# Spreading the last chunk's layer-1 tiles among the remaining layer-2 tiles in a two-layer dense graph kernel

## What is computed

```python
h = relu(layernorm(x))
mask = (adj < 0.5) & ~eye
S = where(mask, exp(-(1/r - 1/mu)**2 / (2*sigma**2)), 0)      # r = adj where mask, else 1
x = x + S @ (h @ W0 + B0)
h = relu(layernorm(x))
out = x + (adj*adj + eye) @ (h @ W1.T)
```

## Time and profile before

| | |
|---|---|
| median of 3 executions | 1946.03 us (1943.99 to 1946.5) |
| profiled execution | 1945.05 us, span 1943.3 us |
| PE / DVE / ACT / POOL busy, share of the span | 97% / 86% / 86% / 4% |
| mean granted TensorE clock | 0.994 of full speed |
| moved by DMA | 487.60 MB, mean 251 GB/s |
| layer-2 tiles: own / in chains; `adj` loads | 94 / 162; 418 |

### The profile page before, as it was taken

One profiled execution on the slowest core, in us unless ns is written; L12 is line 12 of the kernel. 1 busy time (PEld: TensorE's weight loads), 2 busy tenths in 40 slices (PEclk: granted clock), 3 DMA queues, 4 the chain that ended last, 5 costly groups with the idle time before them and its releaser, 6 DMA issues.

```text
span 1943.3 us, 12915 instructions
## 1 busy us (share of the span) xinstructions
PE 1876.0 (97%) x4576; PEld 842.4 (43%) x4576; DVE 1666.1 (86%) x937; ACT 1674.8 (86%) x963; POOL 83.0 (4%) x157
## 2 busy tenths in 40 slices
PE   6988989999999999999999999999999999999998
PEld 4543333344444444444444444444444444444443
DVE  7998999999999999999999999999999994333344
ACT  7999999999999999999999999999999994222221
POOL 0000000000000101010000000000000000000000
PEclk9999999999999999999999999999999999999999
DMA  7565676777787777776656564546564646889885
GB/s 269 190 233 204 249 279 243 256 268 270 265 318 297 294 286 293 288 275 246 257 216 227 207 226 178 218 175 241 205 240 153 227 173 249 313 335 323 329 326 195
DMA packets 77744, 487.60 MB, mean 251 GB/s; under 512 B 9968, under 2 KB 10352, under 8 KB 24176
## 3 DMA queue, kind: packets, MB, share of 16 engines
q1 hardware_dynamic: 65520, 446.92, 62.7%
q0 software_dynamic: 12160, 39.86, 5.6%
HBM read 464.72 MB, written 22.02 MB: 250 GB/s over the span
## 4 chain that ended last, share of the span: by engine, by line
ACT 65%; PE 24%; DVE 5%; issue 5%; DMA 1%; DVEq 0%; POOLq 0%; POOL 0%; SPq 0%
ACT rings L617 21%; ACT rings L627 20%; ACT rings L622 19%; PE p_x L369 17%; ACT rings L634 3%; PE p_l1b L355 3%; PE p_own L369 2%; DVE rings L495 2%; DVE rings L502 2%; DVE rings L513 1%; PE p_l1a L355 1%; DMA x_buf<-xT 1%; ACT rstd_buf L663 0%; ACT rstd_buf L661 0%; ACT square_buf L655 0%
## 5 line engine op out<-in xcount | busy, mean ns | idle before, releaser
L502 DVE SCALAR_TENSOR_TENSOR rings<-rings,small 128x2048 f32<-128x2048 f32 x256 | 600.9, 2347 | 58.8 <-ACT rings L622 58.0
L495 DVE SCALAR_TENSOR_TENSOR rings<-rings 128x2048 f32<-128x2048 f32 x256 | 585.3, 2286 | 0.6
L369 PE MATMUL p_x<-rings,h 128*128 128x512 f32 x1296 | 568.5, 592 | 0.1
L627 ACT ACTIVATE rings<-rings,small 128x2048 f32<-128x2048 f32 x256 | 532.6, 2080 | 4.1 <-DVE rings L502 4.1
L513 DVE TENSOR_TENSOR rings<-rings 128x2048 f32<-128x2048 f32 x174 | 397.9, 2287 | 147.0 <-PE p_x L369 146.6
L617 ACT ACTIVATE rings<-rings,small 128x2048 f32<-128x2048 f32 x256 | 509.0, 1988 | 7.6 <-DVE rings L495 6.9
L355 PE MATMUL p_l1b<-rings,h 128*128 128x512 f32 x1024 | 465.4, 599 | 27.8 <-ACT rings L627 27.8
L622 ACT ACTIVATE rings<-rings 128x2048 f32<-128x2048 f32 x256 | 487.9, 1906 | 4.9
L355 PE MATMUL p_l1a<-rings,h 128*128 128x512 f32 x1024 | 464.1, 598 | 12.5 <-ACT rings L627 12.5
L369 PEld LDWEIGHTS p_x<-rings,h 128*128 128x128 f32 x1296 | 246.3, 190 | 309.6 <-issue 309.1
L369 PE MATMUL p_own<-rings,h 128*128 128x512 f32 x752 | 338.3, 593 | 0.3
(11 more groups left out here) (69 smaller groups left out, 307.4 us busy)
## 6 DMA issues: line engine op xcount, KB each, us to landing
rings<-adjT SPq DMA_DIRECT2D x418, 1024.0 KB, 5.4
xa_buf<-acc_dram POOLq DMA_DIRECT2D x57, 256.0 KB, 6.5
acc_dram<-xa_buf POOLq DMA_DIRECT2D x52, 256.0 KB, 5.4
x_buf<-xT SPq DMA_DIRECT2D x32, 256.0 KB, 5.2
outT<-xa_buf POOLq DMA_DIRECT2D x16, 256.0 KB, 3.8
acc_dram<-y_buf POOLq DMA_DIRECT2D x15, 256.0 KB, 5.5
y_buf<-acc_dram POOLq DMA_DIRECT2D x11, 256.0 KB, 6.1
acc_dram<-x_buf POOLq DMA_DIRECT2D x1, 256.0 KB, 5.5
```

The costliest lines, as they stand in the source:

```text
L369: last = pe.matmul(out[:, :], h2[:, it.source * G + g, :], block_of(q_ring, it.m % Q_RING, g), start=(it.first and g == 0), stop=(it.last ...
L495: dve.scalar_tensor_tensor(out=tile(s_ring, t % S_RING), in0=tile(a_ring, slot), scalar=CUTOFF, in1=tile(a_ring, slot), op0=ALU.is_lt, op1 ...
L502: dve.scalar_tensor_tensor(out=v, in0=v, scalar=neg_2c, in1=v, op0=ALU.add, op1=ALU.mult).then_inc(squared, 1)
L627: act.activation(v, v, ACT.Exp, bias=exp_bias, scale=neg_k).then_inc(sens_done, 1)
```

## The change

Four things. The quotas of chunks 1 to 14 add up to 157 instead of 152. In the last chunk nearly all that is left goes among the sixteen layer-1 tiles: 65 items, four or five a step, three more (TAIL) right behind. The 31 tiles of sources 14 and 15 form the final chains, two tiles each (one for row 15); the first four are open together in four banks (`p_x[0]`, `p_x[1]`, `p_own[0]`, `p_l1[0]`), first their tiles of source 14, then those of source 15, and later ones use these four banks in turn. From the last chunk on ACT and DVE square in turn, and the steps between the layers come ahead of the squares. A chain is added after the DVE's part of the item three behind its last (one behind in final chains), and POOL's transfers are sorted by item instead of by step. The plan has 72 chains instead of 68, 90 own tiles instead of 94, 422 loads instead of 418; 17 chains end in chunks 4 to 8 instead of 30. ACT squares 39 items in chunks 1 to 14 instead of 37, DVE 19 in chunks 1 to 3 instead of 15.

```diff
-QUOTA = [0, 4, 7, 9] + [12] * 12
+QUOTA = [0, 5, 9, 11] + [12] * 11
+TAIL = 3
+OPEN = 4
+EVAC = 3
+STEAL = 0.5
...
+def slots_of(c):
+    if c == 1:
+        n = QUOTA[1]
+        return [H2_STEP + k * (NC - H2_STEP) // n for k in range(n)]
+    if c < NC - 1:
+        n = QUOTA[c]
+        return [(2 * k + 1) * NC // (2 * n) for k in range(n)]
+    n = NC * NC - 2 * NC + 1 - sum(QUOTA) - TAIL
+    return [(2 * k + 1) * NC // (2 * n) for k in range(n)] + [NC + k for k in range(TAIL)]
...
+    ends = [Chain(row, [J for J in range(NC) if (row, J) not in done], True) for row in range(NC)]
+    chains += ends
+    tail = [(ch, ch.sources[0]) for ch in ends[:OPEN]] + [(ch, ch.sources[1]) for ch in ends[:OPEN]]
+    tail += [(ch, J) for ch in ends[OPEN:] for J in ch.sources]
+    items += [Item(ch.row, J, ch, S_STEPS + TAIL + k) for k, (ch, J) in enumerate(tail)]
+    for k, ch in enumerate(chains):
+        ch.index = k
+        ch.bank = (k - len(chains) + NC) % OPEN if ch.final else k % 2
...
-    if it.step >= S_STEPS:
+    if it.step >= S_STEPS - NC:
         it.by = "act" if it.m % 2 else "dve"
...
+for ch in CHAINS:
+    ch.evac = max(ch.last_m + (1 if ch.final else EVAC), CHAINS[ch.index - 1].evac if ch.index else 0)
+    ch.store = ch.evac + 0.5
+    EVAC_AFTER.setdefault(min(ch.evac, len(ITEMS) - 1), []).append(ch)
+    TRANSFERS.append((ch.store, 0, ch.index))
+    if state_before(ch) is not None:
+        free = CHAINS[ch.index - XA_RING].store if ch.index >= XA_RING else 0
+        free = max([free, ch.first_m - 1] + [o.store for o in ch.before])
...
+        TRANSFERS.append((free, 1, ch.index))
+    ch.after = [o for o in CHAINS[:ch.index] if o.bank == ch.bank]
...
+        p_chain = p_x + [p_own[0], p_l1[0]]
...
-                elif it.first and it.chain.index >= 2:
-                    pe.wait_ge(xa_added, it.chain.index - 1)
+                elif it.first and it.chain.final and it.chain.bank == 2 and it.chain.row < OPEN:
+                    pe.wait_ge(y_ready, NC - 2)
+                elif it.first and it.chain.final and it.chain.bank == 3 and it.chain.row < OPEN:
+                    pe.wait_ge(x1_added, NC - 1)
+                elif it.first and it.chain.after:
+                    pe.wait_ge(xa_added, it.chain.after[-1].index + 1)
...
+                if c >= NC - 1:
+                    row_steps(c, i)
                 for it in AT_STEP[s]:
                     if it.by == "dve":
                         square_adj(it)
+                    for ch in EVAC_AFTER.get(it.m, []):
+                        add_chain(ch)
```

More of the change, by code:

```diff
@@ L23, with __init__ @@
 TINY = 2.0 ** -60
-QUOTA = [0, 4, 7, 9] + [12] * 12
+QUOTA = [0, 5, 9, 11] + [12] * 11
 S_STEPS = NC * NC
 H2_STEP = 9
+TAIL = 3
+OPEN = 4
+EVAC = 3
+STEAL = 0.5
 class Chain:
-    def __init__(self, index, row, sources, final):
-        self.index, self.row, self.sources, self.final = index, row, sources, final
+    def __init__(self, row, sources, final):
+        self.row, self.sources, self.final = row, sources, final
 class Item:
@@ L42, in __init__, with next_chain @@
         self.own = chain is None
-def best_row(c, limit, done):
+def slots_of(c):
[7 more added lines that the diff above has]
+    return [(2 * k + 1) * NC // (2 * n) for k in range(n)] + [NC + k for k in range(TAIL)]
+def next_chain(c, places, done):
     found = None
+    late = places[0] >= H2_STEP
+    limit = c if late and c < NC - 1 else c - 1
     for row in range(NC):
+        if row == c or row == c - 1 and not late:
+            continue
         left = [J for J in range(limit) if (row, J) not in done]
-        if row in (c - 1, c) or not left:
+        if not left:
             continue
-        key = (row < c, len(left), -row if row < c else row)
+        key = -(STEAL * (row > c) + 1 / len(left)), -row if row < c else row
         if found is None or key > found[0]:
@@ L54, in best_row @@
     return found
[L57 to L66, removed]
-def make_plan():
[L70 to L80, removed]
-            chains.append(chain)
[L82 to L94, removed]
-        rest = iter(J for J in range(NC) if J not in own)
[L96 to L106, removed]
@@ new lines, in make_plan @@
+def make_plan():
+    done, chains, items, order = set(), [], [], [list(range(NC))]
+    for c in range(1, NC):
+        places = slots_of(c)
+        own = [J for J in range(c) if (c, J) not in done][-len(places):]
+        steps = sorted({i for i in places if i < NC})
+        own_at = {steps[(2 * k + 1) * len(steps) // (2 * len(own))]: J for k, J in enumerate(own)}
+        own_at.pop(max(own_at))
+        own_at[NC - 1 if NC - 1 in steps else steps[-1]] = own[-1]
+        done.update((c, J) for J in own)
+        free, picked, taken = [], [], set()
+        for i in places:
+            if i in own_at and i not in taken:
+                taken.add(i)
+                picked.append((i, c, own_at[i], None))
+            else:
+                free.append(i)
+        while free:
+            _, row, left = next_chain(c, free, done)
+            left = left[:len(free)]
+            chain = Chain(row, left, False)
+            chains.append(chain)
+            done.update((row, J) for J in left)
+            picked += [(i, row, J, chain) for i, J in zip(free, left)]
+            free = free[len(left):]
+        rest = iter(J for J in range(NC) if J not in own)
+        order.append([own_at[i] if i in own_at else next(rest) for i in range(NC)])
+        picked.sort(key=lambda p: p[0])
+        items += [Item(row, J, chain, c * NC + i) for i, row, J, chain in picked]
+    ends = [Chain(row, [J for J in range(NC) if (row, J) not in done], True) for row in range(NC)]
[6 more added lines that the diff above has]
+        ch.bank = (k - len(chains) + NC) % OPEN if ch.final else k % 2
@@ L107, in make_plan @@
     return chains, items, order
 CHAINS, ITEMS, ORDER = make_plan()
-STEPS = S_STEPS + len([it for it in ITEMS if it.step >= S_STEPS])
+STEPS = ITEMS[-1].step + 1
 AT_STEP = [[] for _ in range(STEPS + 8)]
@@ L149 @@
     mine = [it for it in ITEMS if it.chain is ch]
-    ch.begin, ch.end, ch.last_m = mine[0].step, mine[-1].step, mine[-1].m
+    ch.begin, ch.end, ch.first_m, ch.last_m = mine[0].step, mine[-1].step, mine[0].m, mine[-1].m
     ch.before = [x for x in CHAINS[:ch.index] if x.row == ch.row]
@@ L179, with first_item @@
 PRIORS = [c for c in range(NC) if prior_of(c) is not None]
+EVAC_AFTER, TRANSFERS = {}, []
+for ch in CHAINS:
[6 more added lines that the diff above has]
+        free = max([free, ch.first_m - 1] + [o.store for o in ch.before])
+        if ch.begin >= (ch.row + 1) * NC:
+            free = max(free, [it.m for it in ITEMS if it.step >= (ch.row + 1) * NC + 4][0] + 0.2)
+        assert free <= ch.evac, (ch.row, ch.sources, free, ch.evac)
+        TRANSFERS.append((free, 1, ch.index))
+    ch.after = [o for o in CHAINS[:ch.index] if o.bank == ch.bank]
+def first_item(step):
+    return [it.m for it in ITEMS if it.step >= step][0]
+for c in range(NC):
+    TRANSFERS.append((first_item(NC * (c + 1) + 4) + 0.1, 2, c))
+    if c in PRIORS:
+        TRANSFERS.append((first_item(NC * c + 13), 3, c))
+TRANSFERS.sort()
 def gnn_program(nc, xT, adjT, W0, B0, mu, sigma, W1T, outT):
@@ L335, in _ @@
                     load_residual(c)
[L336 to L340, removed]
+                if s < S_STEPS and S_LOAD[s] >= n:
+                    load_tile(S_LOAD[s])
+                    n = S_LOAD[s] + 1
+                for it in AT_STEP[s]:
+                    if it.load >= n:
+                        load_tile(it.load)
+                        n = it.load + 1
                 if 2 <= s < NC:
@@ L580, in add_chain, with row_steps @@
                     dve.wait_ge(xa_loaded[k % XA_RING], 16 * loads)
-                    dve.tensor_tensor(buf[:, :], p_x[k % 2][:, :], buf[:, :], ALU.add).then_inc(xa_added, 1)
+                    dve.tensor_tensor(buf[:, :], p_chain[ch.bank][:, :], buf[:, :], ALU.add).then_inc(xa_added, 1)
+            def row_steps(c, i):
+                if c > NC:
+                    return
+                if i == 3:
+                    add_x1(c - 1)
+                if i == 4 and c >= 2:
+                    add_y(c - 1)
+                if i == 7:
+                    norm_row(c - 1)
             for s in range(STEPS + 8):
@@ L597, in _ @@
                         constants()
[L598 to L607, removed]
+                if 1 <= c < NC - 1:
+                    row_steps(c, i)
         @block.scalar
@@ L668, in keep_h2, with row_steps @@
                                ACT.Copy).then_inc(h2_ready, 1)
+            def row_steps(s):
+                c, i = divmod(s, NC)
+                if i == 5 and c <= NC:
+                    square_row(c - 1)
+                if i == 6 and c <= NC:
+                    rstd_row(c - 1)
+                if i == 8 and c < NC or s == S_STEPS + 7:
+                    keep_h2(c - 1)
             for s in range(STEPS + 8):
```

(11 more changed lines are left out.)

6 lines of the change are left out of this document (4 added, 2 removed).

## The result

The changed kernel takes **1930.02 us** (median of 6 executions, 1929.39 to 1930.87) against 1945.99 for the kernel before (now six executions, 1943.99 to 1946.5): a ratio of 0.9919, interval 0.9908 to 0.993, 16.0 us less. The forecast was 1928.3, with a range of 1923.5 to 1936. The profiled execution took 1930.87 us (span 1929.1), the slowest of the six.

A forecast was written before the change was run, and what follows sets the result against it. ScalarE was taken to pace the chunks up to the last and TensorE the rest; -18.5 (late part) + 0 (final pairs) + 0 (state transfers) + 0.8 (early chunks) = -17.7 us, forecasting 1928.3 us, range 1923.5 to 1936.

The forecast's parts named there:

- What bounds: Whole kernel: ScalarE paces the chunks up to the last, TensorE the rest.
- The late part: Layer-1 tile 238 to the last matmul: 425.4 us becomes 406.9, five tiles (17.2) and 1.4 us idle, 18.5 less.
- The covers costed at nothing: Last chunk: squares, row work and h2 copy stay hidden behind TensorE; a failed cover costs up to 3 us, once.
- The final pairs: Chains of two tiles at the end: VectorE's add and square cost nothing; bound 7.6 us for eleven chains.
- State transfers: POOL's chain state loads cost nothing: 12.2 us free against a median landing of 6.7 us.
- rivals 1 and 3: 1: transfers bound final pairs, about 1934 us, chance 0.11; 3: late state loads stall VectorE, near 1954 us, 0.07.
- The early chunks: Chunks 1 to 14: two more ScalarE squares +3.6, fewer waits for VectorE -2.8, net +0.8 us.
- A sign in between: Periods between h2 copies up to 960 us should be 98 to 100.3 us; over 101 would show rival 2.
- rival 2: Early chunks give the gain back, VectorE or chain waits holding ScalarE: 5 to 10 us, 1933 to 1938; chance 0.07.
- The tail: Behind the last matmul: an add, a store and its landing, 6 us of the span, unchanged.

The follow-up runs named there:

- the second read: Changed kernel with VectorE copying the bank once more ahead of each of the last eleven chains' adds: 1934.98 us, ratio 0.9943.
- Quotas alone: Kernel before with only its quotas for chunks 1 to 3 raised from 4, 7, 9 to 4, 9, 11: 1935.76 us, ratio 0.9947.
- 159 tiles: Changed kernel with quotas 5, 10, 12 for chunks 1 to 3, 159 tiles before the last chunk instead of 157: 1951.45 us, ratio 1.0028.

## Why the prediction was right, point by point

- **What bounds.** ScalarE before the last chunk, TensorE after. Eleven more ScalarE squares cost 18.3 us. It does not hold the other way: with fewer of them VectorE holds ScalarE, so VectorE is close behind. Fewer tiles left for the end is what pays: all else changed, the five tiles bring 14.7 us (1944.72 to 1930.02), and four of them alone, in the kernel before, 10.0.
- **The late part, -18.5.** -18.3: 407.1 us measured against 406.9 worked out; before 425.4. With its parts: five tiles, and the idle time that spreading takes away (408.5 us without it).
- **The covers costed at nothing.** Squares, row work and banks: TensorE idle 0.12 us in 407. ScalarE's copy of h2 for row 15 began at 1825.98 us, ScalarE's square behind it ended at 1828.4 and the first tile that needs both began at 1829.2: about 0.9 us to spare, as 3.4 against 2.5 had said.
- **The final pairs, 0.** Right, with the reason given: the second read showed the margin, about 0.1 us, and the price of 0.6 us more, 0.47 us a pair.
- **State transfers, 0, and rivals 1 and 3.** Landings rose from 6.7 to 7.6 us, as more is carried, against 12.2 free. Rival 1 had the load right and came near: with 382 GB/s asked for, the pairs ran at 380 GB/s with a share of 0.99, above the 367 that it took as its bound, and the `adj` loads landed in 8.6 us instead of the 6.8 of the earlier trace rows. TensorE never waited all the same. How much was to spare no run shows: the share says little, the 429 GB/s of the earlier trace rows some 50 GB/s. The Trainium skill, "DMA: Bandwidth & Descriptors", section "Where 436 GB/s comes from", has the HBM side bind at about 358 GB/s; the trace does not agree, for it shows 380 over 57 us. Its "HBM Reference", section "Specifications (TRN2)", has a core that streams alone measure well above that share, and the trace agrees with that.
- **The early chunks, +0.8: measured +1.5.** Measured as the start of tile 238, the profiles differ by +3.15 us. Of it +1.63 is the first copy of h2 (164.62 before, 166.25 after), which is no effect: the code is the same up to there, the same kernel run again had 165.30, and the one with the second read 164.76. That leaves +1.52, in four parts. (1) ScalarE's squares: two more up to tile 238, as forecast, +3.6. (2) VectorE's holding of ScalarE was mis-sized: it fell by about 3.8 us (what is left of the +2.46 between the first and the fourteenth copy once three squares and part 3 are taken off), not by 2.8. How much of it would go was a guess between bounds, and that it came near is luck. (3) A term that the sum lacks, +1.0: ScalarE's `log` is followed by a square or a step of the row after 1.89 us and by `reciprocal` after 2.02, and the latter happens 149 times instead of 141, since on the new positions the square of position 8 shares its `log` with the copy of h2. Steady chunks take 100.05 us instead of 99.89, with three squares in each. That it goes with the positions and not with the new code is borne out by the run with the old quotas: its squares are back on 4, 10 and 15, and four of its chunks take 99.89 us (the other steady ones 100.4). (4) Behind the fourteenth copy the changed kernel has one ScalarE square fewer, but 0.7 us less come back than that is worth; the chain that ended last runs on TensorE there already, from 1477.12 us.
- **A sign in between.** The periods up to 960 us were to be 98 to 100.3 us, and over 101 would have spoken for rival 2. Four were 98.4 to 100.1, one 100.81, with a wait of 0.45 us for VectorE in it.
- **The tail, 0.** From the last add to the end of the span 7.0 us instead of 6.0. Quotas alone, whose end is as before, has 7.0 as well, so it is not the pairs; the other runs have 6.6 to 8.4. It stays open what it is.
- In the profiles these make -18.3 + 3.15 + 1.0 = -14.2, which is 1945.05 to 1930.87. The medians differ by 16.0: the profiled execution lies 0.9 us under its median before and 0.9 us over it after.
- **Rival 2** (the early chunks give it back) fell for these quotas, but it is what decides at others. Nobody had chosen that with 157 tiles ScalarE's squares fall on 3, 8 and 14, and the forecast does not look at positions: that part is luck, and a chance of 0.07 was too small for it. The same sums over a chunk gave 1924 to 1928 us for 159 tiles, which take 1951.

## What to carry to other kernels

When one engine paces the first part of a kernel and another the second, spreading within the second gains next to nothing (1.4 us here); what counts is how much of the second engine's work fits beside the first part, and it can be priced by tiles left. Here sums of busy time over a chunk told what is impossible but not what will fit: where two engines hand each tile back and forth, a rule such as "every fourth" should be tied to positions in the chunk, not to a running number, and be tried at more than one phase. Before a wait is called free, put a second copy of the work ahead of it and read how much is absorbed.

## What was not expected

- Three squares of each chunk on positions 0, 6, 11 instead of 3, 8, 14 cost some 2 us of 100 in each steady chunk, 18 us in all, though ScalarE had two squares fewer to do.
- Moving 15 squares from the fullest engine (199 of 200 us) to one with 3 to 4% of room made the kernel 12 us slower.
- Kernels that are alike up to their first copy of h2 reached it between 164.62 and 166.25 us: a single profile can be off by a tenth of this change.
